# Cross-attention and routed feed-forward on one core: which half of the stacked queries a row score waits for, and where the mask is prepared

## The reference

```
x = x + cross_attention(layernorm(x), context, mask)   # 16 heads of 8
x = x + mixture_of_experts(layernorm(x))               # 8 experts, 2 chosen for a token, capacity-limited
```

## Time and profile before

| | us |
|---|---|
| median of 3 runs (lowest, highest) | 427.91 (425.01, 429.54) |
| the profiled execution | 425.72 |
| its span, first to last instruction | 423.9 |

### The profile page before, as it was taken

The page is one execution under the profiler, slowest core; times in us unless marked ns, Lnnn a source line. Parts: engine busy times, 40 slices in busy tenths (PEclk is TensorE's granted clock), DMA queues, the critical chain, the costliest instruction groups (busy, mean ns, idle before and its releaser), DMA issues.

```text
span 423.9 us, 8967 instructions
## 1 busy us (share of the span) xinstructions
PE 364.0 (86%) x3012; PEld 313.7 (74%) x3012; DVE 251.7 (59%) x934; ACT 194.6 (46%) x438; POOL 229.6 (54%) x195
## 2 busy tenths in 40 slices
PE   5877788878788888875789999999999999999990
PEld 2565566656566566544579999999999999999980
DVE  6677776778676686676033556555555655555530
ACT  2566555656565565553033344334444433444320
POOL 6542331071864555577505638567483855838674
PEclk9999888989898898895889999999999999999996
DMA  8994101121222211112142353725446372544232
GB/s 252 306 320 166 15 6 16 30 54 39 57 65 53 84 44 46 47 57 66 47 126 20 28 155 33 163 28 90 102 38 157 31 160 28 97 92 39 26 32 25
DMA packets 41158, 34.33 MB, mean 81 GB/s; under 512 B 8336, under 2 KB 37520, under 8 KB 40976
## 3 DMA queue, kind: packets, MB, share of 16 engines
q1 hardware_dynamic: 26592, 23.40, 19.0%
q0 software_dynamic: 13568, 9.58, 16.4%
q10 hardware_dynamic: 960, 0.87, 0.7%
HBM read 21.12 MB, written 17.73 MB: 92 GB/s over the span
## 4 chain that ended last, share of the span: by engine, by line
PE 71%; ACT 11%; DVE 6%; issue 4%; POOL 4%; DMA 2%; POOLq 0%; SPq 0%; DVEq 0%; ACTq 0%
PE bank L913 16%; PE bank L671 10%; PE bank L773 9%; PE bank L673 9%; PE bank L672 9%; PE bank L741 5%; PE bank L764 3%; ACT qs L540 3%; POOL slots L440 3%; ACT qs L535 3%; PE bank L790 2%; PE bank L904 2%; ACT logd L559 1%; DVE mneg L1024 1%; ACT guess L564 1%
## 5 line engine op out<-in xcount | busy, mean ns | idle before, releaser
L472 POOL DMA_INDIRECT out<-ys,idx x80 | 125.5, 1569 | 83.8 <-DVE ys L1302 47.0
L1329 DVE TENSOR_TENSOR h<-sg,bank 128x256 f32<-128x256 f32 x160 | 66.2, 418 | 87.5 <-ACT sg L656 79.7
L656 ACT ACTIVATE sg<-bank 128x256 f32<-128x256 f32 x160 | 61.5, 385 | 108.3 <-PE bank L673 107.4
L671 PE MATMUL bank<-ex_hi,w_hi 128*128 128x256 f32 x320 | 96.0, 300 | 1.1 <-DVE ex_lo L1283 0.2
L673 PE MATMUL bank<-ex_lo,w_hi 128*128 128x256 f32 x320 | 89.7, 280 | 0.0
L672 PE MATMUL bank<-ex_hi,w_lo 128*128 128x256 f32 x320 | 89.7, 280 | 0.0
L913 PE MATMUL bank<-w_raw,h 128*128 128x128 f32 x640 | 78.0, 275 | 0.8 <-DVE h L1329 0.8
L913 PEld LDWEIGHTS bank<-w_raw,h 128*128 128x128 f32 x640 | 74.8, 192 | 1.0 <-DVE h L1329 1.0
L440 POOL DMA_INDIRECT slots<-rall,slot x64 | 62.8, 981 | 18.1 <-issue 17.7
L671 PEld LDWEIGHTS bank<-ex_hi,w_hi 128*128 128x128 f32 x320 | 61.0, 191 | 4.1 <-issue 2.5
L672 PEld LDWEIGHTS bank<-ex_hi,w_lo 128*128 128x128 f32 x320 | 61.0, 191 | 0.0
(11 more groups left out here) (122 smaller groups left out, 555.1 us busy)
## 6 DMA issues: line engine op xcount, KB each, us to landing
slots<-in_empty SPq DMA_DIRECT2D x8, 660.0 KB, 10.1
xl<-slots SPq DMA_DIRECT2D x7, 660.0 KB, 7.3
w_raw<-in_wgu SPq DMA_DIRECT2D x8, 512.0 KB, 3.8
w_raw<-in_wdn SPq DMA_DIRECT2D x8, 256.0 KB, 4.2
out<-X SPq DMA_DIRECT2D x16, 128.0 KB, 1.9
X<-in_x SPq DMA_DIRECT2D x3, 512.0 KB, 7.1
out<-ys,idx POOLq DMA_INDIRECT x80, 3.3
slots<-rall,slot POOLq DMA_INDIRECT x64, 2.3
```

The source lines that it names most:

```text
L472: nc.gpsimd.indirect_dma_start(out=out[:, :], out_offset=bass.IndirectOffsetOnAxis(ap=IDX[v][:, j:j + 1], axis=0), in_=YS[c][:, t, :], in_ ...
L656: nc.scalar.activation(SG[m % 2][:], GATE_PS[m % 2][:, 0:2 * P], ACT.Silu).then_inc(sg_ready, 1)
L671: nc.tensor.matmul(ps, hi, m_hi, start=True, stop=False)
L1329: nc.vector.tensor_tensor(H[n % 2][:, f, :], SG[m % 2][:], UP_PS[m % 2][:, 0:2 * P], ALU.mult).then_inc(h_ready, 1)
```

## The change

The first row score of a batch waits for the first copy of its stacked queries, the second row score for the second. The cast of MASKT moves from VectorE to ScalarE, ahead of ScalarE's conversion of the key weights. VectorE's two operations on MASKR move behind the subtraction that gives WK_LO. The second run of `keep_warm` has one matmul more.

```diff
-WARM0 = (4, 7)
+WARM0 = (4, 8)
...
             nc.scalar.preload_act_table_set("natural_log_exp_and_others")
+            act.wait_ge(maskt_in, 16)
+            nc.scalar.copy(MASKB[:], MASKT[:]).then_inc(maskb_ready, 1)
             act.wait_ge(wk_in, 16)
...
                 t, bank = m // 2, m % 2
+                if m < 2:
+                    pe.wait_ge(qs_ready, 2 * b + 1 + m)
                 if m == 0:
-                    pe.wait_ge(qs_ready, 2 * b + 2)
                     if b < KBUF:
...
             nc.vector.memset(QS[0][ONE_ROW:ONE_ROW + 1, :, :].bitcast(F32), 1.0).then_inc(v2_first, 1)
-            dve.wait_ge(maskt_in, 16)
-            nc.vector.tensor_copy(MASKB[:], MASKT[:]).then_inc(maskb_ready, 1)
-            dve.wait_ge(maskr_in, 16)
-            nc.vector.tensor_reduce(ANYR[:], MASKR[:], AX.X, ALU.max).then_inc(anyr_ready, 1)
-            nc.vector.tensor_scalar(EXT[:], MASKR[:], -1.0, BIG, ALU.add, ALU.mult).then_inc(ext_step, 1)
             dve.wait_ge(count_full, 1)
...
             nc.vector.tensor_tensor(WK_LO[:], WK[:], WK_HI[:].bitcast(F32), ALU.subtract).then_inc(wk_lo_ready, 1)
+            dve.wait_ge(maskr_in, 16)
+            nc.vector.tensor_reduce(ANYR[:], MASKR[:], AX.X, ALU.max).then_inc(anyr_ready, 1)
+            nc.vector.tensor_scalar(EXT[:], MASKR[:], -1.0, BIG, ALU.add, ALU.mult).then_inc(ext_step, 1)
             dve.wait_ge(anyr_ready, 1)
```

## The result

The changed kernel takes **399.34 us** in the median of 4 runs (395.59 to 399.81), the kernel before 427.97 us (4 runs, 425.01 to 429.54). The ratio is 0.932 with an interval of [0.924, 0.940]. The profiled execution took 399.12 us, with a span of 397.3 us against 423.9, so 26.6 us went between these two traces. I follow the time from row score 0 of one batch to that of the next ("a step"), as the prediction does.

What follows compares the result with a forecast made beforehand. Bound: TensorE idle before row score 0 for ScalarE's stacked queries. 25.7 - 1.8 - 0.5 - 2.3 = 21.1, 28.7 with the clock; 425.7 - 28.7 = 397.0, as median 399 us; range 394 to 410.

Steps and rivals of the forecast that it cites:

- The wait of row score for line 535: TensorE's idle wait before row score 0 for ScalarE's stacked queries, 27.2 us; 25.7 won and not moved to row score 1.
- The clock term: First part: nine falls to 1.2 GHz behind TensorE's gaps go with the gaps, 7.6 us won; lower end 0.
- the clock falls as before: Rival: TensorE's granted clock still falls in the first part despite the removed gaps; 407 us, chance 0.25.
- GpSimd's part: Two steps where GpSimd's deviation, behind its sends, is late keep part of the wait: 1.6 and 0.7, 2.3 us lost.
- VectorE's hand-over: VectorE's round of 7.43 against TensorE's 7.37 makes it late, 0.14 a step over 13 steps: 1.8 us lost.
- the statistics' 0.5: Three quick steps with statistics of the next tiles: VectorE's round about 8.3 against TensorE's 8.1, 0.5 us lost.
- Step 0 and the start: Start edits counted 0, first values waiting for the gate's load (14.3 us); ahead of batches 2 and 1, 1.6 and 0.8 won.
- The tail: Behind the last row score nothing changes, GpSimd's last 12 sends keep their distance; the last clock fall counts 1.3 us.
- Sends that stretch: Rival: denser VectorE holds each GpSimd send by about 0.25, steps of five sends grow to 8.4; 403 us, chance 0.07.
- a clock near 1 between 49 and 180 us: Sign of being right: TensorE's granted clock near full over that stretch of the first part.
- about 125 us for the 15 steps: Sign of being right: the 15 steps between row scores 0 take about 125 us instead of 153.
- 10 and 11 us for the held ones: Sign of being right: two steps held by GpSimd's deviation take 10 and 11 us.

Runs made afterwards that it cites:

- e1: Kernel before with only the split wait on the stacked queries, mask edits and extra warming matmul left out; 432.86 us, ratio 0.966, on a chip with pauses.
- f3: Kernel before with seven matmuls on constants in TensorE's rest ahead of row score 0, every wait kept; 417.92 us, ratio 0.980, on the quiet chip.
- f4: Changed kernel with 8 and 13 matmuls on constants filling TensorE's two long rests ahead of second transpositions; 392.39 us, 0.920 of the kernel before.
- g3: Changed kernel with GpSimd's sends dealt out anew and small loads WO and GATE issued before three large X loads; 431.71 us, 0.968 of the kernel before.
- g4: Changed kernel with sends dealt out anew and the last ten second-expert sends left out; 426.1 us, 0.957 of the kernel before, chip with pauses.
- f2: Changed kernel with GpSimd's sends of steps 5 to 10 dealt out as 2, 5, 2, 5, 5, 5; 388.39 us, 0.909 of the kernel before.
- e2: Changed kernel with the old wait for both halves put back, so only the start's edits; 448.46 us, ratio 1.005 to the kernel before, chip with pauses.

## Why the prediction came out right, point by point

The forecast was 399, the result 399.34. The mechanism is shown; but part of the match is luck, since two sizes were off and cancelled.

- **The wait of row score for line 535** (25.7 of 27.2 us won, and not moved): right. No such row is left beyond 0.21 us, and score 1 never waits for the second half after batch 0. e1 shows that this edit alone makes the steps up to 77 us.
- **The clock term, 7.6 us**: right in cause, and near in size as the price of the old falls: f3 gives 7.9 by the medians with nothing else removed, and 9.5 in steps 1 to 14. (Three of the falls that the prediction put at 1.2 us each are worth 1.5 there: 10.82, 10.75 and 10.76 us become 9.31, 9.26 and 9.27.) But the change itself won hardly any of it, since new falls cost 7.2 us (next point). The rival "the clock falls as before" (407) is excluded where it put the falls, since none stands behind a row score 0 any more; but elsewhere nearly as much slow time came back. What I had not followed to its end is my own sentence that every fall stands behind a rest: it holds for the rests that stay. By the rule of the Trainium skill that the prediction named ("TensorE: Matmul & The Clock Gate", Part 1), that activity releases the lower clock, the full term was to come. The trace of f3 agrees with it from step 1 on; in the changed kernel two rests were enough to lose most of the term again.
- **GpSimd's part, 2.3 us**: mis-sized, the largest miss. The rests are as counted: the two steps would have 9.4 and 10.4 us at full clock (f4), where the prediction said "10 and 11". But the prediction took 0.3 and 0.4 of clock as won there, while the clock fell for longer than before, at a cost of 7.2 us in this execution. The three steps 7 to 9 take 34.97 us; the prediction's terms make 28.3 (31.48 of before, less 3 x 1.79, plus 2.3 for GpSimd and 0.6 for VectorE, less 0.7 of clock). That is +6.7.
- **VectorE's hand-over, 1.8 us, and the statistics' 0.5**: not paid. The 0.14 a step was mis-summed as well: the round of 7.43 less TensorE's 7.37 is 0.06, and no row shows the "free at 131.5". Steps 10 to 14 take 36.13 us where the terms make 38.9 (50.75 less 5 x 1.79 and 3 x 1.2, plus 5 x 0.14), and steps 1 to 6 take 47.48 instead of 49.6 (61.12 less 1.6, 5 x 1.79 and 2.0 of clock, plus 1.05 for VectorE): -4.9 together, of which 0.9 are the three falls at 1.5 instead of 1.2. I had measured VectorE's round from its first instruction to its last (7.43) and so counted small pauses, in which it waited, as work. Its busy time in that step was 7.24, and a plain step takes 7.20 to 7.36. TensorE's 7.37 held 0.1 of slower start behind the rest as well: row score 0 took 0.50 there and takes 0.40 now.
- **Step 0 and the start**: the sum had 0 for the start and 0.8 won in step 0. The first score starts 0.8 earlier (19.45), and step 0 takes 10.49 instead of 9.58, since TensorE is at 1.2 GHz from 23.1 to 26.4 us: +1.7 and -0.8. The start's rows are as reasoned: the mask's cast takes 0.20 us on ScalarE (1.74 on VectorE before), the masked context starts at 5.85, the keys' projection at 8.63, and still the first values at 14.65, behind a rest of 0.87. g3 names the bound, the gate's load. The rows, of ScalarE, VectorE and TensorE:

```profile
3.49 0.20 ACT L488 CAST maskb<-maskt 64x16 bf16<-64x16 int32 x1
```

```profile
5.85 0.69 DVE L968 TENSOR_TENSOR ctxm<-ctx,any 128x512 f32<-128x512 f32 x1 [1.70 <-DMA ctx<-in_ctx]
```

```profile
8.63 0.74 PE L673 MATMUL bank<-ctx_hi,wk_hi 128*96 128x512 f32 x1 [1.16 <-DVE ctx_lo L974]
...
14.65 1.09 PE L702 MATMUL bank<-wv,ctx 128*64 128x128 f32 x16 [0.87 <-issue]
```

- **The tail**: 1.9 us gone, 1.3 counted (the clock behind the last score). The last 12 sends follow the last deviation as the prediction said (166.90 to 181.96, before 193.32 to 208.38: 15.06 us both times). New is that this deviation starts straight behind a send (0.55 us of waiting before), and that GpSimd has had hardly a rest since 126 us (0.2 to 0.4 us now and then): the backlog of sends sets when the tiles are placed. It hides well: g4 gives 2.6 us for ten of them.
- **Sends that stretch** (403): excluded. The page's mean of the 64 sends is 983 ns (before 981), with VectorE full in the steps. Of the effect that the prediction cited for this rival ("SBUF — State Buffer" of the Trainium skill, the box on descriptor starvation) this kernel shows nothing; whether any of VectorE's operations here runs in the two-port mode that the box speaks of, no run shows.

The misses of the profiled execution add up: +1.7, -2.1, +6.7 and -2.8 in the steps, -0.8 ahead and -0.6 behind them = +2.1, that is 26.6 us won instead of 28.7. The median came out at 399 all the same: the long steps, too short by 6.7 in the sum, were nearly paid by the other steps, and the profiled execution lies 0.2 below the median after, where it lay 2.2 below before.

Of the signs that the prediction named, three did not come: a clock near 1 between 49 and 180 us (it is 0.72 and 0.65 in two of the steps), about 125 us for the 15 steps (129.07), and 10 and 11 us for the held ones (12.41 and 14.53). Plain steps are shorter than its 7.6 to 7.8 (7.20 to 7.36).

What stays open: whether the start's edits cost something (ratios 1.005 and 1.016 on chips with pauses; the rest ahead of the first values), what the pauses of those chips are, and why a rest of the same length is followed by a fall in one execution and not in another.

## What to carry to other kernels

When a wait is taken off the busiest engine, list the rests that remain on it and price each with what the clock does behind it, not by its length alone: here two rests, which lengthen their steps by 5.3 us, brought up to 7.2 us of slow work. Once nobody waits, the next bound is an engine that works in order with unrelated work ahead of what the others need (GpSimd's sends ahead of a deviation); dealing that work out anew won 9.8 us more (f2) without removing any. And for the round of an engine take its busy time, not the distance between its first and its last instruction, as long as it still waits within.

## What the runs showed of the hardware that was not expected

- Rests of TensorE of 1.91 and 2.97 us were followed by 1.2 GHz until 87.9 and 111.8 us, that is for 6.7 and 9.1 us of matmuls from its first one behind the rest (81.23, 102.72). In another execution of the same kernel 1.98 us of rest were followed by none, e2 has three rests of 1.79 us at full clock, and in the kernel before four of 13 such rests brought no fall.
- Matmuls on a constant whose results nobody reads made two kernels faster: 7.9 us with seven in each of 15 steps (f3), and 398.15 to 392.39 with 21 in all (f4; the intervals of the ratios touch, the runs don't).
- An indirect DMA occupies GpSimd for 0.96 us and 0.30 until the next, beside a VectorE that rests or that is 100% busy.
- Chips differ in more than speed: on two of the chips the kernel before took 447 and 453 us instead of 426 to 428, and the kernels traced there have the same lengths of steps 1 to 6 as elsewhere up to about 77 us, where no fall of the clock lengthens them, and pauses of 1 to 6 us in the steps behind (the longest 5.74, e2).
